# One attention kernel, one change: the output projection of an image spread one quarter at a time, and its group statistics by one selection product

## The chip, the cores and the metric

The kernel runs on one core of one Trainium2 chip. The metric is device time in microseconds (us) of one execution. The engines are TensorE (PE; its weight loads are PEld), VectorE (DVE), ScalarE (ACT), GpSimd (POOL) and SyncE (SP, which issues most DMAs). Each engine works through its own queue in order; they wait for one another by semaphores.

## The reference, cut to what matters

Eight images of 64 channels, 64 x 64. Four directional scans come first (not touched here). Then one attention layer:

```python
xn = group_norm(x, gn1_w, gn1_b)            # 32 groups of 2 channels
q, k, v = split(conv1x1(xn, w_qkv))         # 4 heads of 32
q, k = elu(q) + 1, elu(k) + 1
kv, k_sum = k^T v, sum of k                 # per head
out = (q kv) / (q . k_sum + 1e-6)
out = conv1x1(out, w_out)
out = group_norm(out, gn2_w, gn2_b)         # mean and variance over 2 channels x 64 x 64
return out + residual
```

The last group norm is what the change is about. A group is 2 channels; on the chip an image lies on 128 partitions (channel, and which half of the image), so the statistics of a group are spread over four partitions.

## The kernel before, in words

The scans end some 447 us into the program. Then comes a software pipeline of eight passes, one per image, by `iteration(b, par, cur, prev, pp)` on every engine (`batches` runs passes 0, 1, 2, a loop over 3 to 6, and 7), and a tail written out by hand. Pass b makes keys, queries and values of image b, denominators and outputs of image b-1 and, two behind, outputs and the last group norm of image b-2. The order on each queue is the order of the code; nothing else schedules it. Each pass has four quarters (i = 0 to 3), and a quarter is one chunk of 512 columns.

TensorE, per quarter: `token_major` (L595), `keys` (L603, L609), `queries` (L617, L621); one quarter later `gather` (L635) and `key_sums` (L641). In quarter 0 also `sums` (L650, L653) and `denominators` (L690). `output(c, cpar, i)` (L701) projects chunk i of image c; it needs the query units 2i and 2i+1 divided by their denominators (semaphore `normed`). Pass b runs outputs 2 and 3 of image b-2 in quarter 0, one on either side of `denominators`, and outputs 0 and 1 of image b-1 in quarter 3. `group_sums` (L666) adds the statistics over the four partitions of a group; it runs twice an image (mean, then variance), as `small(b, 3)` and `small(b, 4)`.

ScalarE: `tokens` (L1340), the exponentials of keys (L1374) and queries (L1380), `collect` (L1359), which copies a finished output chunk out of PSUM, `high_of` (L1335), and `affine` (L1394), the scale and shift of the last group norm over a whole image, in quarter 0 behind the collects.

VectorE: keys and queries finished (L1014, L1024), `small` (den_w and mix L1031/L1032, den L1036, reciprocal L1039), `normalise` (L1005), `low_half` (L287, two per pass, both at the end), `output_stats` (bn_stats L1063, two at a time) and the aggregate (L1057), and in `small(b, 3)` and `small(b, 4)` the deviations and the variance (L1044 to L1051).

SyncE: `broadcast(c, m)` writes the reciprocals of half m of image c to DRAM (`bounce`, L375) and reads them back over all partitions (four copies of 256 KB, L381). It issues the copies only when all units of image c-1 have been multiplied (`normed`).

GpSimd: `finish` (L479, residual added; waits for `affine`), `normalise_units` (L458, four units of 512 columns, first for half 0, then for half 1; each waits for its broadcast), `scale_and_shift` (L462, L466, L473: the inverse root, times weight, shift). "First units" below are those of half 0, "second units" those of half 1.

Of the kernel before, what the change touches and what calls it, by code (L numbers as in the profile page):

```python
# [53 lines left out]
SUBS = 4  # L54
SUB = CHUNK // SUBS
# [17 lines left out]
def constants():  # L73

    p = np.arange(P)
    head = p // DH
    group = (p % C) // 2
    row = np.arange(SUBS * DH)
    places = SUBS * head[:, None] + (row // DH)[None, :] == (row % DH)[None, :]

    sub, to = np.divmod(np.arange(SUBS * P), P)
    back = (p % DH)[:, None] == (SUBS * head[to] + sub)[None, :]
    return np.concatenate([np.eye(P), head[:, None] == head[None, :], (group[:, None] == group[None, :]) / 4.0,
                           places, back], axis=1).astype(np.float32)


def build(nc, x, k_td, k_dt, k_lr, k_rl, gn1_w, gn1_b, w_qkv, w_out, gn2_w, gn2_b, consts, out):
    with ExitStack() as ctx:
# [51 lines left out]
        back_to_heads = scan_rows[:, 0:SUBS * P].rearrange("p (s n) -> p s n", s=SUBS)  # L140
        back_ps = (key_ps[0], key_ps[1], query_ps[0], query_ps[1], acc_ps, out_ps, key_ps[0], tok_ps)
# [42 lines left out]
        dev2 = sb("dev2", [P, 4])  # L184
# [43 lines left out]
        normed_last, back_loaded, back_done = sem("normed_last"), sem("back_loaded"), sem("back_done")  # L228
        tail_done, tail_read = sem("tail_done"), sem("tail_read")
# [39 lines left out]
        def small_step(b, n):  # L269


            if isinstance(b, int):
                return n + 1 if b == 1 else 5 * b - 6 + n
            return b * 5 + (n - 6)
# [37 lines left out]
        def _(sp):  # L312
# [76 lines left out]

            for c in range(2):  # L390
                for m in range(2):
                    broadcast(c, m)
            sp.dma_start(back_to_heads, consts[:, 3 * P + SUBS * DH:].rearrange("p (s n) -> p s n", s=SUBS))\
# [25 lines left out]
        def _(pool):  # L419
# [41 lines left out]
            def scale_of_output(b, par):  # L461
                nc.gpsimd.tensor_tensor(scale2[:, par:par + 1], dev2[:, 1:2], half[:, 0:1], ALU.pow)\  # L462
# [6 lines left out]
            def scale_and_shift(b, par):  # L469
                scale_of_output(b, par)  # L470
                at_least(pool, scale_ready, 2 * b)
                settled(pool)
                nc.gpsimd.tensor_scalar(shift2[:, par:par + 1], dev2[:, 3:4], scale2[:, par:par + 1],  # L473
# [11 lines left out]
            def iteration(b, par, cur, prev, pp):  # L485
# [28 lines left out]
            pool.wait_ge(tail_read, 5)  # L514
# [6 lines left out]
            pool.wait_ge(tail_read, 7)  # L521
# [5 lines left out]
        def _(pe):  # L527
# [135 lines left out]
            def group_sums(v):  # L663
                for h in range(HEADS):
                    here = slice(h * DH, (h + 1) * DH)
                    last = nc.tensor.matmul(small_ps[here, 0:1], group_mean[:, here], v, start=True, stop=True)  # L666
                return last

            def small(b, n):
# [9 lines left out]
                if n >= 3:  # L679

                    at_least(pe, stat_ready, 2 * (b - 2) + n)
                    last = group_sums(agg2[:, 0:1] if n == 3 else dev2[:, 2:3])
# [22 lines left out]
            def iteration(b, par, cur, prev, pp):  # L705
                for i in range(4):
# [5 lines left out]
                    if i == 0 and prev:  # L712
                        small(b, 0)
                        if pp:
                            output(b - 2, par, 2)
                        else:
                            image_mean(0, REST, out_ps, rest_stat_ready, rest_stat_done)
                        denominators(b, par, 0)
                        if pp:
                            output(b - 2, par, 3)  # L720
                    if i > 0:
                        gather(b, i - 1)
                        if i == 3 and prev and has_next(b, cur):

                            at_least(pe, small_read, small_step(b, 0))
                            if not pp:
                                pe.wait_ge(rest_shift_ready, 1)
                            output(b - 1, 1 - par, 0)
# [5 lines left out]
                    if i == 3:  # L734
                        if pp:
# [726 lines left out]
```

## Time and profile before

| what | us |
|---|---|
| median of 3 runs | 667.25 (667.12 to 667.75) |
| the profiled execution | 667.11 |
| its span in the trace | 665.0 |
| the scans, up to pass 0 | about 447 |
| passes 1 to 7 | 466.3 to 635.0 |
| the tail | 635.0 to 665.0 |

Passes are told by ScalarE's first copy of the pass (acc_g, tok, L1345/L1340). The view by stretches gives, for each pass, its length, the busy time of each engine in it and TensorE's granted clock; the timeline gives single instructions with the idle time ahead of them and what ended it.

### The profile page before, as it was taken

The numbers are of one execution on the slowest core, as the hardware profiler recorded it, in microseconds if no ns is written. First come the engines' busy times: TensorE is split into PE (matmuls) and PEld (weight loads), VectorE is DVE, ScalarE is ACT, GpSimd is POOL, SyncE is SP. The second block draws the span as 40 slices with busy tenths as digits, with TensorE's granted clock in tenths as the row PEclk, the third lists the DMA queues.
The fourth block names the chain that finished last, engine by engine and source line by source line (L and its number), as shares of the span: only waits on it lengthen the run. The fifth ranks groups of instructions, "written<-read, shape, count | busy, mean of one in ns | idle before, by whom it ended". The sixth has DMA issues, their size and how long they took to land.

```text
span 665.0 us, 28191 instructions
## 1 busy us (share of the span) xinstructions
PE 624.7 (94%) x10787; PEld 535.6 (81%) x10787; DVE 568.4 (85%) x1945; ACT 430.2 (65%) x1062; POOL 135.2 (20%) x116
## 2 busy tenths in 40 slices
PE   8799999999999999999999999998989899899991
PEld 5799999999999899999999999965646555555550
DVE  5689989999989888989999999989878768778785
ACT  3456666677777766666665666657767767768744
POOL 0022200000000000000000000010164767767655
PEclk9999999999999999999999999999999999999996
DMA  9999990233333100000000000000326368368556
GB/s 173 206 203 189 166 178 1 51 82 80 80 79 83 41 1 0 0 0 0 0 2 0 0 0 0 0 1 2 73 69 148 78 134 177 90 132 178 111 91 130
DMA packets 79315, 50.40 MB, mean 76 GB/s; under 512 B 44256, under 2 KB 72352, under 8 KB 79264
## 3 DMA queue, kind: packets, MB, share of 16 engines
q1 hardware_dynamic: 75936, 48.91, 36.4%
q10 hardware_dynamic: 3328, 0.82, 0.6%
q8 instruction: 31, 0.51, 0.3%
q14 instruction: 20, 0.16, 0.1%
HBM read 32.34 MB, written 9.24 MB: 63 GB/s over the span
## 4 chain that ended last, share of the span: by engine, by line
PE 51%; DVE 19%; issue 10%; DMA 7%; POOL 6%; ACT 2%; SPq 1%; DVEq 1%; ACTq 0%; POOLq 0%
PE bank L554 44%; POOL rows_h L458 6%; DMA rows_h<-bounce 5%; DVE scan_rows L860 5%; DVE parts L860 3%; DVE parts L833 3%; DVE fin L947 3%; DMA bounce<-recip 1%; PE bank L635 1%; PE bank L701 1%; SPq L381 1%; DVE kp L1014 1%; DVE rows_h L1024 1%; DMA yn<-L_conv_k_td 1%; DVE recip L1039 1%
## 5 line engine op out<-in xcount | busy, mean ns | idle before, releaser
L554 PE MATMUL bank<-parts 128*128 128x124 f16 (+2 forms) x7560 | 421.3, 219 | 6.9 <-issue 3.7
L554 PEld LDWEIGHTS bank<-parts 128*128 128x128 f16 x7560 | 415.6, 98 | 13.0 <-issue 4.8
L1235 ACT ACTIVATE parts<-parts 128x128 f16<-128x128 f16 x506 | 156.6, 309 | 150.1 <-DVE parts L860 125.5
L833 DVE TENSOR_TENSOR parts<-scan_rows,parts 128x128 f16<-128x128 f32 x506 | 149.3, 295 | 14.2
L860 DVE SCALAR_TENSOR_TENSOR parts<-bank,cols_w 128x128 f16<-128x128 f32 x378 | 109.6, 290 | 21.7 <-PE bank L554 6.2
L860 DVE SCALAR_TENSOR_TENSOR scan_rows<-bank,cols_w 128x128 f32<-128x128 f32 x378 | 106.1, 281 | 0.0
L443 POOL TENSOR_TENSOR scale<-dev,half 128x2 f32<-128x2 f32 (+1 forms) x2 | 2.1, 1037 | 398.9 <-DVE dev L972 398.9
L458 POOL TENSOR_TENSOR rows_h<-rows_h 128x512 f32<-128x512 f32 x52 | 69.6, 1370 | 43.2 <-DMA rows_h<-bounce 43.2
L1014 DVE SCALAR_TENSOR_TENSOR kp<-ex,bank 128x512 f32<-128x512 f32 x64 | 41.0, 681 | 28.0 <-ACT ex L1374 27.5
L1246 ACT ACTIVATE cols_w<-scan_rows 128x256 f32 x126 | 52.5, 417 | 5.7 <-issue 0.2
L1374 ACT ACTIVATE ex<-bank,minus_one 128x512 f32<-128x512 f32 x64 | 40.5, 687 | 7.5 <-PE bank L609 7.1
L1380 ACT ACTIVATE ex<-bank,minus_one 128x512 f32<-128x512 f32 x64 | 40.7, 695 | 1.1 <-PE bank L621 1.1
L1024 DVE SCALAR_TENSOR_TENSOR rows_h<-ex,bank 128x512 f32<-128x512 f32 x64 | 40.9, 681 | 0.0
L860 DVE SCALAR_TENSOR_TENSOR parts<-bank,rows_h 128x128 f16<-128x128 f32 x124 | 36.0, 290 | 5.4 <-PE bank L554 0.4
L635 PEld LDWEIGHTS bank<-kp,tok 128*64 128x64 f32 x512 | 27.3, 136 | 11.3 <-issue 10.6
L1359 ACT ACTIVATE rows_h<-bank 128x512 f32<-128x512 f32 x26 | 15.6, 600 | 31.4 <-PE bank L701 29.2
L635 PE MATMUL bank<-kp,tok 128*64 128x128 f32 x512 | 35.0, 279 | 0.1
L860 DVE SCALAR_TENSOR_TENSOR scan_rows<-bank,rows_h 128x128 f32<-128x128 f32 x124 | 34.8, 281 | 0.0
L1262 ACT ACTIVATE cols_w<-ex 128x128 f32 (+1 forms) x84 | 34.0, 414 | 0.6 <-DMA ex<-scan_rows 0.5
L701 PE MATMUL bank<-rows_h,mix 128*64 128x512 f32 x96 | 25.4, 605 | 5.7 <-POOL rows_h L458 5.7
L947 DVE BATCH_NORM_STATS2 fin<-cols_w x96 | 28.8, 300 | 0.0
L1246 ACT ACTIVATE rows_h<-scan_rows 128x256 f32 (+1 forms) x64 | 26.7, 416 | 2.2
(143 smaller groups left out, 575.7 us busy)
## 6 DMA issues: line engine op xcount, KB each, us to landing
rows_h<-bounce SPq DMA_DIRECT2D x52, 256.0 KB, 4.9
cols_w<-x SPq DMA_DIRECT2D x6, 896.0 KB, 12.5
ex<-scan_rows SPq DMA_DIRECT2D x84, 64.0 KB, 2.0
out<-fin SPq DMA_DIRECT2D x10, 512.0 KB, 7.8
cols_w<-x SPq DMA_DIRECT2D x12, 384.0 KB, 9.2
cols_w<-x SPq DMA_DIRECT2D x12, 256.0 KB, 7.0
cols_w<-x SPq DMA_DIRECT2D x6, 512.0 KB, 10.7
kp<-scan_rows SPq DMA_DIRECT2D x40, 64.0 KB, 2.0
```

What stands on the lines that cost most here:

```text
L458: nc.gpsimd.tensor_tensor(qp[:, 1 - par, u, :], qp[:, 1 - par, u, :], recip_b[:, u, :], ALU.mult).then_inc(normed, 1)
L554: last = nc.tensor.matmul(conv_rows[g][u % SLOTS][:, :, to], w[:, k, d, :], rows_16[:, u % SLOTS, g * GB:(g + 1) * GB, of], start=part_n = ...
L635: nc.tensor.matmul(acc_ps[d * C:(d + 1) * C, 0:P], tok[:, i % 2, n * P + d * C:n * P + (d + 1) * C], kp[:, (2 * i + d) % 4, n * P:(n + 1) ...
L833: nc.vector.tensor_tensor(low[:, slot, gb, :], state[:, slot, gb, :] if row is None else row[:, gb, :], high[:, slot, gb, :], ALU.subtract ...
L860: nc.vector.scalar_tensor_tensor(out=to, in0=conv[g][u % SLOTS][:, 0:GB * J].rearrange("p (b j) -> p b j", b=GB), scalar=0.0, in1=add, op0 ...
L947: nc.vector.bn_stats(stats[:, b, bass.ds(n * 2 + (g - 2), 1), :].rearrange("p o s -> p (o s)"), cols[:, bass.ds(n * -BODY + (W + first), c ...
L1014: nc.vector.scalar_tensor_tensor(out=kp[:, m % 4, :], in0=ex[:, m % 2, :], scalar=1.0, in1=key_ps[m % 2][:, :], op0=ALU.min, op1=ALU.max)\
L1024: nc.vector.scalar_tensor_tensor(out=qp[:, par, u, :], in0=ex[:, 2 + u % 2, :], scalar=1.0, in1=query_ps[u % 2][:, :], op0=ALU.min, op1=AL ...
L1235: act.activation(high_down[:, slot, gb, :], high[:, slot, gb, :], ACT.Copy, scale=1.0 / LOW_SCALE).then_inc(down_ready[g], 1)
L1246: act.activation(to, state[:, slot, :, :], ACT.Copy).then_inc(saved, 1)
L1374: act.activation(ex[:, m % 2, :], key_ps[m % 2][:, :], ACT.Exp, bias=minus_one[:, :])\
L1380: act.activation(ex[:, 2 + u % 2, :], query_ps[u % 2][:, :], ACT.Exp, bias=minus_one[:, :])\
```

## The change

Six things change, all in the attention passes and the tail.

1. Outputs: pass b now runs output 0 of image b-1 in quarter 3, and outputs 1, 2 and 3 of image b-2 in quarters 0, 1 and 2 (before: 2 and 3 in quarter 0, 0 and 1 in quarter 3). The collects move with them. In quarter 3 both gathers stand ahead of both key sums.
2. Statistics: instead of two `group_sums` with VectorE work between them, `members()` multiplies the 24 columns of `stats2` (four bn_stats of six numbers) by four 0/1 matrices (`pick`), 16 matmuls of 24 columns, so that each partition gets all four members' bn_stats side by side in PSUM (96 numbers). One bn_aggr over the 96 (`joined`) gives mean and variance of the group; two one-column instructions make variance + eps and -mean.
3. GpSimd: `scale_and_shift` stands ahead of the second units. Its wait is for VectorE's two one-column results (`stat_ready`), which come at the end of the pass.
4. ScalarE: `affine` stands behind the exponentials of quarter 1 (before: of quarter 0).
5. VectorE: one `low_half` at the end of quarter 2, one at the end of quarter 3; bn_stats of chunks 0 and 1 in quarter 1 ahead of the second denominators, chunk 2 in quarter 2, chunk 3 in quarter 3 ahead of the queries.
6. One more DMA (`pick`, 256 KB) is issued by SyncE after the first image's broadcasts, and the tail uses `members` and `joined` in the place of the two sums.

```diff
+    member, to = np.divmod(np.arange(MEMBERS * P), P)
+    pick = p[:, None] == ((to % C) // 2 * 2 + member % 2 + member // 2 * C)[None, :]
...
             def scale_of_output(b, par):
-                nc.gpsimd.tensor_tensor(scale2[:, par:par + 1], dev2[:, 1:2], half[:, 0:1], ALU.pow)\
+                at_least(pool, stat_ready, 2 * b - 1)
+                nc.gpsimd.tensor_tensor(scale2[:, par:par + 1], dev2[:, 0:1], half[:, 0:1], ALU.pow)\
...
                 if prev:
                     normalise_units(b, par, 0)
+                if pp:
+                    scale_and_shift(b, par)
                 if prev and has_next(b, cur):
                     normalise_units(b, par, 1)
-                if pp:
-                    at_least(pool, small_read, small_step(b, 4))
-                    scale_and_shift(b, par)
...
-            def group_sums(v):
-                for h in range(HEADS):
-                    here = slice(h * DH, (h + 1) * DH)
-                    last = nc.tensor.matmul(small_ps[here, 0:1], group_mean[:, here], v, start=True, stop=True)
+            def members():
+                for j in range(MEMBERS):
+                    for h in range(HEADS):
+                        here = slice(h * DH, (h + 1) * DH)
+                        last = nc.tensor.matmul(small_ps[here, j * NCHUNK * 6:(j + 1) * NCHUNK * 6], pick[:, j, here],
+                                                stats2[:, :, :].rearrange("p n s -> p (n s)"), start=True, stop=True)
                 return last
...
+            def joined(b, read, n):
+                settled(dve)
+                nc.vector.bn_aggr(agg2[:, :], small_ps[:, 0:MEMBERS * NCHUNK * 6]).then_inc(read, 1)
+                at_least(dve, read, n)
+                at_least(dve, affine_ready, b - 1)
+                nc.vector.tensor_scalar(dev2[:, 0:1], agg2[:, 1:2], EPS_GN, None, ALU.add).then_inc(stat_ready, 1)
+                nc.vector.tensor_scalar(dev2[:, 1:2], agg2[:, 0:1], -1.0, None, ALU.mult).then_inc(stat_ready, 1)
...
+                    if i >= 2 and prev and has_next(b, cur):
+                        low_half(dve, b + 1, 1 - par, i - 2)
+                    if i == 3 and pp:
+                        small(b, par, 3)
...
                     if i == 0 and pp:
-                        collect(b - 2, par, (2, 3))
-                    if i == 0 and has_finished(b):
+                        collect(b - 2, par, (1,))
+                    if i == 1 and has_finished(b):
                         affine(b - 1, 1 - par, slice(0, J))
...
+                    if i in (1, 2) and pp:
+                        collect(b - 2, par, (i + 1,))
                 if prev and has_next(b, cur):
-                    collect(b - 1, 1 - par, (0, 1))
+                    collect(b - 1, 1 - par, (0,))
```

Where it moves instructions, at the three places that matter below. Line numbers are each kernel's own; ISA and REGISTER_ALU rows are semaphore and counter work.

GpSimd in the loop, one pass, before (fin: the residual; rows_h: units; scale, shift: the group norm's):

```order
L479 TENSOR_TENSOR fin<-rows_h,cols_w 128x64x32
L243 ISA
L458 TENSOR_TENSOR rows_h<-rows_h 128x512 x8
L243 ISA
L462 TENSOR_TENSOR scale<-dev,half 128x1
L243 ISA
L466 TENSOR_SCALAR scale<-scale,norm 128x1
L473 TENSOR_SCALAR shift<-dev,scale,norm 128x1
```

The same place now:

```order
L491 TENSOR_TENSOR fin<-rows_h,cols_w 128x64x32
L249 ISA
L468 TENSOR_TENSOR rows_h<-rows_h 128x512 x4
L249 ISA
L473 TENSOR_TENSOR scale<-dev,half 128x1
L477 TENSOR_SCALAR scale<-scale,norm 128x1
L485 TENSOR_SCALAR shift<-dev,scale,norm 128x1
L468 TENSOR_TENSOR rows_h<-rows_h 128x512 x4
```

The eight units are parted: the scale and shift stand between the first four and the second four.

ScalarE in the loop, from the first collect of a pass on, before (rows_h<-bank: a collect; 128x2048: the affine; tok and ex: tokens and exponentials):

```order
L1359 ACTIVATE rows_h<-bank 128x512
L243 REGISTER_ALU
L1359 ACTIVATE rows_h<-bank 128x512
L1394 ACTIVATE rows_h<-rows_h,shift,scale 128x2048
L243 REGISTER_ALU
L1340 ACTIVATE tok<-bank 128x512
L243 REGISTER_ALU
L1374 ACTIVATE ex<-bank,minus_one 128x512
L243 REGISTER_ALU
L1374 ACTIVATE ex<-bank,minus_one 128x512
L1380 ACTIVATE ex<-bank,minus_one 128x512 x2
```

The same place now:

```order
L1334 ACTIVATE rows_h<-bank 128x512
L249 REGISTER_ALU
L1315 ACTIVATE tok<-bank 128x512
L249 REGISTER_ALU
L1349 ACTIVATE ex<-bank,minus_one 128x512
L249 REGISTER_ALU
L1349 ACTIVATE ex<-bank,minus_one 128x512
L1355 ACTIVATE ex<-bank,minus_one 128x512 x2
L1371 ACTIVATE rows_h<-rows_h,shift,scale 128x2048
L249 REGISTER_ALU
L1334 ACTIVATE rows_h<-bank 128x512
```

Quarter 1's tokens and exponentials now follow one collect; the affine and the next collect follow them.

TensorE at the end of a pass in the loop, before (kp,tok: gather; rows_h,mix: output; kp,ones: key sums; agg/dev,cst: group sums):

```order
L701 MATMUL bank<-rows_h,mix 64x512 x2
L641 MATMUL bank<-kp,ones 32x256 x4
L243 REGISTER_ALU
L243 ISA
L666 MATMUL bank<-agg,cst 32x1 x4
L243 REGISTER_ALU x2
L635 MATMUL bank<-kp,tok 64x128 x8
L243 REGISTER_ALU
L701 MATMUL bank<-rows_h,mix 64x512 x2
L641 MATMUL bank<-kp,ones 32x256 x4
L243 REGISTER_ALU x2
L666 MATMUL bank<-dev,cst 32x1 x4
```

The same place now:

```order
L712 MATMUL bank<-rows_h,mix 64x512 x2
L249 REGISTER_ALU x2
L643 MATMUL bank<-kp,tok 64x128 x8
L649 MATMUL bank<-kp,ones 32x256 x8
L249 REGISTER_ALU
L675 MATMUL bank<-stats,scan_rows 32x24 x16
```

One output is left there, and the 16 matmuls with `pick` (L675) end the pass.

## Rows read from the trace of the kernel before

**Rows 1.** Stretches by pass (1, 2, 3, 6, 7): length, busy us, clock, DMA.

```profile
core 0: us, PE busy (x) PEld busy (x) DVE busy (x) ACT busy (x) POOL busy (x), PEclk, DMA share, GB/s
466.34:490.23 23.89, 21.64 (x366) 13.52 (x366) 19.43 (x35) 15.48 (x27) 8.51 (x7) 1.00 0.40 95
490.23:512.69 22.46, 22.46 (x386) 13.82 (x385) 18.49 (x34) 16.41 (x28) 9.05 (x8) 1.00 0.47 108
512.69:538.45 25.76, 23.00 (x386) 13.82 (x384) 19.13 (x35) 18.54 (x29) 17.05 (x13) 1.00 0.49 113
...
588.92:613.51 24.59, 22.92 (x386) 13.84 (x384) 19.45 (x35) 18.54 (x28) 17.65 (x13) 1.00 0.60 133
613.51:635.03 21.52, 20.50 (x361) 12.66 (x360) 16.65 (x31) 15.04 (x24) 15.59 (x12) 1.00 0.65 122
```

**Rows 2.** Timeline, GpSimd, pass 5 into 6: start, us, instruction, idle before.

```profile
568.95 0.57 POOL L462 TENSOR_TENSOR scale<-dev,half 128x1 f32<-128x1 f32 x1
...
570.25 1.38 POOL L473 TENSOR_SCALAR shift<-dev,scale,norm 128x1 f32<-128x1 f32 x1 [0.21 <-POOL scale L466]
574.04 4.58 POOL L479 TENSOR_TENSOR fin<-rows_h,cols_w 128x2048 f32<-128x2048 f32 x1 [2.42 <-ACT rows_h L1394]
579.52 4.99 POOL L458 TENSOR_TENSOR rows_h<-rows_h 128x512 f32<-128x512 f32 x4 [0.89 <-DMA rows_h<-bounce]
587.71 5.99 POOL L458 TENSOR_TENSOR rows_h<-rows_h 128x512 f32<-128x512 f32 x4 [3.20 <-DMA rows_h<-bounce]
```

**Rows 3.** Timeline, ScalarE, the same pass, quarters 0 to 1.

```profile
571.66 2.09 ACT L1394 ACTIVATE rows_h<-rows_h,shift,scale 128x2048 f32<-128x2048 f32 x1 [0.86 <-POOL shift L473]
573.66 0.58 ACT L1340 ACTIVATE tok<-bank 128x512 f32<-128x512 f32 x1
```

**Rows 4.** Timeline, VectorE, the same pass: quarter 1 and the end.

```profile
574.84 1.29 DVE L1014 SCALAR_TENSOR_TENSOR kp<-ex,bank 128x512 f32<-128x512 f32 x2 [3.43 <-ACT ex L1374]
...
577.71 0.95 DVE L1039 RECIPROCAL recip<-den 128x128 f32<-128x128 f32 x1
...
586.57 1.22 DVE L287 TENSOR_TENSOR parts<-yn,parts 128x1024 f16<-128x1024 f32 x1
...
588.45 1.61 DVE L287 TENSOR_TENSOR parts<-yn,parts 128x1024 f16<-128x1024 f32 x1
```

**Rows 5.** Timeline, SyncE's DMA issues, passes 2 and 5.

```profile
502.14 0.34 SPq L375 DMA_DIRECT2D bounce<-recip  x1
506.28 1.73 SPq L381 DMA_DIRECT2D rows_h<-bounce  x4
...
580.49 1.73 SPq L381 DMA_DIRECT2D rows_h<-bounce  x4
```

**Rows 6.** Timeline, TensorE: denominators of pass 6, and that pass's end.

```profile
592.39 1.08 PE L690 MATMUL bank<-rows_h,den_w 128*32 128x128 f32 x32
...
609.76 0.64 PE L641 MATMUL bank<-kp,ones 128*32 128x256 f32 x8
610.22 0.22 PE L666 MATMUL bank<-agg,cst 128*32 128x1 f32 x8
610.37 1.09 PE L635 MATMUL bank<-kp,tok 128*64 128x128 f32 x16
```

**Rows 7.** Groups by line and form: VectorE's aggregate of 78 and of 24 numbers.

```profile
L963 DVE BATCH_NORM_AGGREGATE agg<-fin 128x2 f32<-128x78 f32 x8 | 3.3, 469 | 0.0
...
L1057 DVE BATCH_NORM_AGGREGATE agg<-stats 128x2 f32<-128x24 f32 x8 | 2.1, 264 | 1.2 <-DVE stats L1063 0.2 <-DVE stats L1196 0.2
```

**Rows 8.** Timeline, GpSimd, the end of pass 7: scale and shift alone.

```profile
635.56 0.57 POOL L462 TENSOR_TENSOR scale<-dev,half 128x1 f32<-128x1 f32 x1 [1.08 <-DVE dev L1051]
...
636.84 0.33 POOL L473 TENSOR_SCALAR shift<-dev,scale,norm 128x1 f32<-128x1 f32 x1 [0.21 <-POOL scale L466]
```

**Rows 9.** Timeline, TensorE, the end of pass 1: its two outputs.

```profile
484.56 1.08 PE L701 MATMUL bank<-rows_h,mix 128*64 128x512 f32 x4 [0.93 <-POOL rows_h L458]
...
487.99 1.08 PE L701 MATMUL bank<-rows_h,mix 128*64 128x512 f32 x4 [0.76 <-POOL rows_h L458]
```

**Rows 10.** Timeline, VectorE, the tail: last aggregate and last variance.

```profile
652.11 0.26 DVE L1057 BATCH_NORM_AGGREGATE agg<-stats 128x2 f32<-128x24 f32 x1 [0.15 <-DVE stats L1196]
...
653.71 0.16 DVE L1147 TENSOR_SCALAR dev<-bank 128x1 f32<-128x1 f32 x1 [0.36 <-PE bank L666]
```

More of the change, by code:

```diff
@@ L54 @@
 SUBS = 4
+MEMBERS = 4
 SUB = CHUNK // SUBS
@@ L82, in constants @@
     back = (p % DH)[:, None] == (SUBS * head[to] + sub)[None, :]
+    member, to = np.divmod(np.arange(MEMBERS * P), P)
+    pick = p[:, None] == ((to % C) // 2 * 2 + member % 2 + member // 2 * C)[None, :]
     return np.concatenate([np.eye(P), head[:, None] == head[None, :], (group[:, None] == group[None, :]) / 4.0,
-                           places, back], axis=1).astype(np.float32)
+                           places, back, pick], axis=1).astype(np.float32)
 def build(nc, x, k_td, k_dt, k_lr, k_rl, gn1_w, gn1_b, w_qkv, w_out, gn2_w, gn2_b, consts, out):
@@ L678, in small @@
                     last = sums(small_ps)
-                if n >= 3:
-                    at_least(pe, stat_ready, 2 * (b - 2) + n)
-                    last = group_sums(agg2[:, 0:1] if n == 3 else dev2[:, 2:3])
+                if n == 3:
+                    if isinstance(b, int) and b == 2:
+                        pe.wait_ge(pick_loaded, 16)
+                    at_least(pe, norm2, b - 1)
+                    last = members()
                 last.then_inc(small_done, 1)
@@ L714, in iteration @@
                         if pp:
-                            output(b - 2, par, 2)
+                            output(b - 2, par, 1)
                         else:
@@ L718, in iteration @@
                         denominators(b, par, 0)
+                    if i in (1, 2):
+                        gather(b, i - 1)
                         if pp:
[L720 to L728, printed above, removed]
+                            output(b - 2, par, i + 1)
                         key_sums(i - 1)
@@ L734, in iteration @@
                     if i == 3:
+                        gather(b, 2)
+                        if prev and has_next(b, cur):
+                            at_least(pe, small_read, small_step(b, 0))
+                            if not pp:
+                                pe.wait_ge(rest_shift_ready, 1)
+                            output(b - 1, 1 - par, 0)
+                        gather(b, 3)
+                        key_sums(2)
+                        key_sums(3)
                         if pp:
                             small(b, 3)
-                        gather(b, 3)
-                        if prev and has_next(b, cur):
-                            output(b - 1, 1 - par, 1)
-                        key_sums(3)
-                        if pp and has_next(b, cur):
-                            small(b, 4)
             batches(pe, iteration)
```

105 lines of the change are left out of this document (35 added, 70 removed).

## The prediction, made before the changed kernel ran

> **What bounds the kernel now.** I read the stretches by pass first. Passes 3 to 6 last 25.76 us falling to 24.59 (they run from 512.69 to 613.51, 100.82 in all), while pass 2, whose TensorE work is the same, lasts 22.46 with TensorE busy in all of it [rows 1]. So TensorE's queue is worth about 22.5 us a pass, and passes 3 to 6 lose 2 to 3 us each to something that pass 2 lacks. VectorE, with 19.1 to 19.5 us of work, isn't it. The granted clock is 1.00 throughout, so the clock is out of it.
>
> What pass 2 lacks is ScalarE's affine. The timelines, read around it, give a ring. GpSimd ends the second units and starts the group norm's scale at 568.95; the shift ends at 571.63 [rows 2]; the affine runs from 571.66 to 573.75; only then come quarter 1's tokens [rows 3], and VectorE has stood 3.43 us for quarter 1's exponentials; its second reciprocal ends at 578.66 [rows 4]; the copies over the partitions are issued at 580.49 [rows 5]; GpSimd gets them at 587.71 and multiplies until 593.70 [rows 2], where the next scale starts. 593.70 - 568.95 = 24.75 us: scale and shift 2.7, affine 2.0, quarter 1 up to the reciprocal 5.0, the way through DRAM 9.0, units 6.0. That ring, not TensorE, is the pace.
>
> **What the change does to that ring.** It cuts it twice. The affine stands behind quarter 1's exponentials, so the shift no longer holds up that quarter; and the scale stands ahead of the second units. The affine's 2.09 us now lies ahead of quarter 2, where its cover is the 3.43 us that VectorE no longer loses a quarter earlier; with the collect behind it, it may make quarter 2 about a microsecond late, and VectorE has over 3 us a pass to spare against TensorE's 22.5.
>
> **What is late next.** Two candidates.
>
> TensorE: 22.46 us a pass, less two group sums, plus 16 matmuls. A group sum holds the queue from 610.22 to 610.37, 0.15 us, for 4 matmuls (8 records) [rows 6]; four times that is 0.6 us for 16. The other end is the denominators, also 16 matmuls of 32 output rows, but 128 columns wide: 1.08 us [rows 6]. 24 columns lie nearer to one column than to 128; I take 0.8 and keep 0.6 to 1.1. The queue is then 22.46 - 0.3 + 0.8 = 22.95 (22.75 to 23.25).
>
> A new ring through GpSimd. SyncE may issue the first copies of the next image only when all second units are multiplied, and these now stand behind the scale, which waits for VectorE's last instructions of the pass. From the end of the second units: copies until GpSimd starts, 587.71 - 580.49 = 7.2, and 0.2 for SyncE's wake; two first units, half of 4.99, 2.5 [rows 2, 5]; output 0, 1.0 [rows 9]; gather, 1.0, and two key sums, each 0.45 (609.76 to 610.22) [rows 6]; `members` 0.8; aggregate of 96 numbers, on the line through 264 ns for 24 and 469 for 78: 0.54 [rows 7]; variance 0.16 [rows 10]; four hand-overs at some 0.12, 0.5; scale to shift 1.6 (635.56 to 637.17) [rows 8]; second units 5.0. Sum 21.4. It turns in less than TensorE's queue, with 1.5 us to spare.
>
> That spare is what can be lost. VectorE's low part costs 1.22 us alone and 1.61 beside GpSimd's units [rows 4], and those four units take 5.99 there, 4.99 elsewhere; a shift beside VectorE takes 1.38 [rows 2], 0.33 alone [rows 8]. So each meeting of a unit with a low part (or with `normalise`) costs GpSimd 1.0 us. The change puts `normalise` in the second units' stretch and a low part in the first units' stretch. Neither need fall on the ring: a meeting with the last second unit or the third first unit delays nobody in it. The ring is 21.4 with none, 22.4 with one, 23.4 with two.
>
> On this meeting the Trainium skill ("SBUF — State Buffer", section "SBUF: two separate sides") says that VectorE's two-input or fast instructions and GpSimd share a port pair as an exclusive lock: who starts first keeps it, and the other stands fully. The 1.61 and 5.99 us agree (0.4 and 1.0 us of standing). By the page alone every overlap costs the rest of the other's instruction; by the rows, 1.0 us. Either way it speaks against this change, and leads to the second rival.
>
> I take a pass of 23.3 us: TensorE's 22.95 and 0.35 of waits. What in passes 3 to 6 is left of the ring's slack hides the rest: bn_stats moved by quarters, bn_stats ahead of the second denominators (two of them make the second reciprocal 1.2 us later, but the second units wait for the scale anyhow), and both gathers ahead of both key sums (same instructions).
>
> **The queues that are passed.** SyncE: the second half's bounce can now be issued while the first half's copies still fly. In pass 2 that happened: 502.14 to 506.28, 4.1 us until the copies could be issued, against 1.8 from the reciprocal's end (578.66) to 580.49 in pass 5 [rows 4, 5]. It makes a small ring of its own: 0.2 + 7.2 + 1.2 + 0.2 + 7.2 + 5.0 = 21.0 (1.2 being an estimate: bounce behind landed copies), also under TensorE. GpSimd: `finish` (4.58) stands behind the affine and ahead of the first units; it ends before the copies land, as in pass 5 (578.62 against 579.52) [rows 2]. The `pick` load is issued once, in passes where SyncE stands idle: nothing.
>
> **The sum**, against the profiled execution's 667.11 (2.11 us outside its span of 665.0; the median, 667.25, is 0.14 higher).
>
> - Passes 3 to 6: 100.82 becomes 4 x 23.3 = 93.2: -7.6 (91.2 to 97.6: -9.6 to -3.2).
> - Pass 1: the output at 487.99 leaves it, 1.0 us of work and 0.76 of wait: -1.8 [rows 9]. A low part, now at the end of quarter 2, may meet the first units and put the other output off by 1.0. I take -1.6 (-1.8 to -0.8).
> - Pass 2: it had no wait: 0.8 - 0.3 = +0.5 (+0.3 to +0.8).
> - Pass 7: gets a third output, 1.0, and `members` for a group sum, 0.65; its present 1.02 us without TensorE work (21.52 - 20.50) [rows 1] belongs to the old ring and goes: +0.6 (+0.4 to +0.9).
> - Tail: before, 652.11 to 653.87 from aggregate to variance, 1.76 us [rows 10]; now `members` 0.6 to 1.1, hand-overs 0.5, aggregate 0.54, variance 0.16: 1.8 to 2.3. The same step before it has cover in the last image's multiplications. +0.2 (0 to +0.5).
>
> -7.6 - 1.6 + 0.5 + 0.6 + 0.2 = -7.9: **659.2 us**. With the bounds of the forecast alone: 656.4 (all good ends) to 662.9 (23.8 a pass and all poor ends).
>
> **The rivals.**
>
> *TensorE isn't short at all.* The Trainium skill ("Perfetto Trace Analysis", section "Identifying the Most-Contended Engine") warns that TensorE's matmul busy share is no good measure of how near the limit it is, and wants the weight loads' share. That share is 13.82 of 22.46 us in pass 2 [rows 1]. If the 22.46 were a pace set by others, passes could come down to VectorE's 19.1 to 19.9. Against it: pass 2 shows TensorE without a single wait, which an engine that follows others doesn't show. It would give 4 x 20.5 = 82: 648. Chance 0.02.
>
> *The new ring sets the pace.* Two meetings and the 1.1 us `members`: 21.4 + 2.0 + 0.3 = 23.7, and a landing or hand-over later by 0.7: 24.4 a pass. 4 x 24.4 = 97.6, -3.2, and -0.3 for the rest: 663.6. For it: GpSimd is busy 17 to 18 us a pass and its queue order puts three waits in one line. Against: the meetings need exact places. Chance 0.20.
>
> *The gain is given back.* The ring at 25.2, as long as the pass now: 667. The scale's wait would have taken the affine's place. Chance 0.09.
>
> *Slower.* One mechanism: the second units, queued on GpSimd behind the wait for the pass's last VectorE instruction, hold back SyncE's first copies, and the first output of the next image holds TensorE. It decides from 25.3 us a pass on. Its price is 21.4 + three meetings, 3.0 (one in the second units, two in the first), + 1.05 for a shift beside VectorE (1.38 against 0.33) + 0.3: 25.8; 4 x 25.8 - 100.82 = +2.4, and -0.3 for the rest: 669.2. Against: the shift comes at the pass's start, some 4 us ahead of `normalise`. Chance 0.08.
>
> **How the numbers follow.** Forecast 0.61, at 659.2; rivals 0.02, 0.20, 0.09, 0.08. The likeliest case's own range is 656.4 to 662.9; to hold 8 in 10 the range takes in the ring at 24.4 with its poor ends: 656.4 to 664.8. About 0.2%, 1.3 us, is what a measurement can tell from no change: faster 0.82, same 0.10, slower 0.08.
>
> **What would show it.** In the changed trace: VectorE's wait of 3.4 us at quarter 1 gone; ScalarE's affine with no wait for the shift; passes 3 to 6 at 23 to 23.6 us with TensorE busy in nearly all; 32 records of the selection matmuls in 0.6 to 1.1 us; the aggregate near 0.54 us; GpSimd idle ahead of the scale (its wait for the pass's end) and the first units starting some 7.4 us after the second units end. I am wrong if TensorE waits over 1 us a pass for the first units at output 0 (the ring), or if VectorE waits for quarter 2's exponentials what it waited for quarter 1's.

## The result, and the profile after

The changed kernel takes 659.47 us (median of 4 runs, 659.12 to 660.12) where the kernel before takes 667.50 beside it: ratio 0.9871, interval 0.9841 to 0.9901. Measured a second time, beside other runs of before, it took 659.24 us, ratio 0.9882 (0.9854 to 0.9911). The forecast was 659.2, from 656.4 to 664.8. Two executions among the experiments below had a far lower mean granted clock (895.23 us at 0.655 in "before, affine in quarter 1", 788.47 us at 0.751 in "outputs and statistics"); the ratios leave them out, and they move those two medians by less than 0.1 us.

The first view is the changed kernel's stretches by pass (1 to 7, then the tail), columns as in [rows 1]:

```profile
core 0: us, PE busy (x) PEld busy (x) DVE busy (x) ACT busy (x) POOL busy (x), PEclk, DMA share, GB/s
468.53:491.40 22.87, 20.27 (x362) 13.54 (x362) 17.82 (x34) 14.87 (x25) 8.64 (x6) 1.00 0.47 110
491.40:514.03 22.63, 22.53 (x402) 14.07 (x402) 19.22 (x30) 16.48 (x28) 10.98 (x8) 1.00 0.47 109
514.03:537.20 23.17, 22.49 (x402) 14.00 (x400) 20.68 (x32) 18.25 (x29) 16.70 (x12) 1.00 0.52 120
537.20:561.08 23.88, 22.52 (x402) 14.07 (x400) 21.60 (x35) 18.24 (x29) 16.73 (x13) 1.00 0.66 141
561.08:584.07 22.99, 22.46 (x402) 13.98 (x400) 20.03 (x30) 18.24 (x29) 16.65 (x12) 1.00 0.66 144
584.07:607.12 23.05, 22.43 (x402) 14.09 (x400) 20.84 (x33) 18.24 (x29) 16.70 (x12) 1.00 0.68 142
607.12:628.03 20.91, 20.70 (x385) 13.01 (x384) 15.29 (x29) 15.62 (x24) 15.31 (x12) 1.00 0.62 121
628.03:657.40 29.37, 15.10 (x304) 7.89 (x290) 20.81 (x38) 13.39 (x20) 15.76 (x16) 0.84 0.65 120
```

Passes 3 to 6 came down from 100.82 us [rows 1] to 93.09, and TensorE is now busy in 22.4 to 22.5 us of each. Set against the forecast's terms, with both profiles of the changed kernel:

| stretch | before | forecast | first profile | second profile |
|---|---|---|---|---|
| up to pass 1 | 466.34 | 0 | +2.19 | +0.45 |
| pass 1 | 23.89 | -1.6 | -1.02 | -1.01 |
| pass 2 | 22.46 | +0.5 | +0.17 | +0.35 |
| passes 3 to 6 | 100.82 | -7.6 | -7.73 | -7.74 |
| pass 7 | 21.52 | +0.6 | -0.61 | -0.60 |
| tail | 29.97 | +0.2 | -0.60 | -0.65 |
| span | 665.0 | | 657.4 (-7.6) | 655.8 (-9.2) |

The profiled executions took 659.15 and 657.62 us, against 667.11 before. The second view is the timeline of pass 5 in the changed kernel (start, us, instruction, idle before it), which answers to [rows 2 to 6]:

```profile
561.05 0.56 POOL L473 TENSOR_TENSOR scale<-dev,half 128x1 f32<-128x1 f32 x1 [1.96 <-DVE dev L1052]
...
562.31 0.34 POOL L485 TENSOR_SCALAR shift<-dev,scale,norm 128x1 f32<-128x1 f32 x1 [0.20 <-issue]
562.60 4.97 POOL L468 TENSOR_TENSOR rows_h<-rows_h 128x512 f32<-128x512 f32 x4
571.99 4.59 POOL L491 TENSOR_TENSOR fin<-rows_h,cols_w 128x2048 f32<-128x2048 f32 x1 [4.41 <-ACT rows_h L1371]
576.60 5.97 POOL L468 TENSOR_TENSOR rows_h<-rows_h 128x512 f32<-128x512 f32 x4
...
569.59 2.11 ACT L1371 ACTIVATE rows_h<-rows_h,shift,scale 128x2048 f32<-128x2048 f32 x1
...
568.58 1.27 DVE L1016 SCALAR_TENSOR_TENSOR kp<-ex,bank 128x512 f32<-128x512 f32 x2
...
573.84 1.28 DVE L1016 SCALAR_TENSOR_TENSOR kp<-ex,bank 128x512 f32<-128x512 f32 x2 [0.32 <-ACT ex L1349]
...
567.53 0.34 SPq L381 DMA_DIRECT2D bounce<-recip  x1
569.34 1.74 SPq L387 DMA_DIRECT2D rows_h<-bounce  x4
573.70 0.34 SPq L381 DMA_DIRECT2D bounce<-recip  x1
576.78 1.73 SPq L387 DMA_DIRECT2D rows_h<-bounce  x4
...
580.14 1.08 PE L712 MATMUL bank<-rows_h,mix 128*64 128x512 f32 x4 [0.40 <-POOL rows_h L468]
...
582.91 0.47 PE L675 MATMUL bank<-stats,scan_rows 128*32 128x24 f32 x32
583.33 0.62 PE L603 MATMUL bank<-ident,parts 128*128 128x128 f16 x8
```

What to see: VectorE's `kp` of quarter 1 (568.58) carries no idle time, where it had 3.43 us [rows 4]; the affine (569.59) waits for nothing, and quarter 2's `kp` (573.84) waits only 0.32 us. (VectorE's longest wait for exponentials is now at quarter 0, 1.85 us at 562.88; TensorE has no marked wait there.) GpSimd waits 1.96 us for VectorE ahead of the scale and 4.41 us for the affine ahead of `finish`, which ends at 576.58, as the first units start. TensorE's only marked wait here is 0.40 us at output 0. The selection matmuls hold the queue from 582.91 to 583.33: 0.42 us.

### The profile page after: what moved, and what is told of

Read it like the earlier page. It is cut to its first block, busy times and chain, and to the rows that moved or that the text cites. A ratio compares the mean times of both kernels' runs of the same rounds, so it can differ in the third digit from the quotient of the medians.

```text
span 657.4 us, 28413 instructions
## 1 busy us (share of the span) xinstructions
PE 620.2 (94%) x10915; PEld 536.1 (82%) x10915; DVE 572.1 (87%) x1929; ACT 429.0 (65%) x1062; POOL 133.5 (20%) x116
## 4 chain that ended last, share of the span: by engine, by line
PE 63%; DVE 16%; issue 8%; POOL 5%; ACT 4%; DMA 2%; DVEq 1%; ACTq 0%; SPq 0%; POOLq 0%
PE bank L562 46%; DVE scan_rows L862 4%; DVE parts L862 3%; DVE fin L949 3%; PE bank L643 2%; PE bank L712 2%; POOL rows_h L468 2%; POOL fin L491 2%; DVE parts L835 2%; PE bank L617 2%; PE bank L649 2%; PE bank L603 2%; PE bank L629 1%; PE bank L701 1%; ACT ex L1349 1%
## 5 line engine op out<-in xcount | busy, mean ns | idle before, releaser
L862 DVE SCALAR_TENSOR_TENSOR parts<-bank,cols_w 128x128 f16<-128x128 f32 x378 | 109.7, 290 | 22.5 <-PE bank L562 7.0
L468 POOL TENSOR_TENSOR rows_h<-rows_h 128x512 f32<-128x512 f32 x52 | 71.7, 1410 | 19.4 <-DMA rows_h<-bounce 19.2
L643 PEld LDWEIGHTS bank<-kp,tok 128*64 128x64 f32 x512 | 28.8, 139 | 15.0 <-issue 13.5
L1315 ACT ACTIVATE tok<-bank 128x512 f32<-128x512 f32 x32 | 19.4, 605 | 15.4 <-PE bank L603 15.4
```

The costliest lines, as they stand in the source:

```text
L468: nc.gpsimd.tensor_tensor(qp[:, 1 - par, u, :], qp[:, 1 - par, u, :], recip_b[:, u, :], ALU.mult).then_inc(normed, 1)
L643: nc.tensor.matmul(acc_ps[d * C:(d + 1) * C, 0:P], tok[:, i % 2, n * P + d * C:n * P + (d + 1) * C], kp[:, (2 * i + d) % 4, n * P:(n + 1) ...
L862: nc.vector.scalar_tensor_tensor(out=to, in0=conv[g][u % SLOTS][:, 0:GB * J].rearrange("p (b j) -> p b j", b=GB), scalar=0.0, in1=add, op0 ...
```

## The experiments

Runs of one kernel scatter by one or two us, in one set by six. Pass 1 began between 465.4 and 468.5 us in the profiles: the first tokens of pass 0 came at 446.6 to 448.6, and pass 0 took 18.4 to 20.4. So beside each median I read two spans from the same trace: from the start of pass 1 to the end, and passes 4 to 6, which ran at full clock in all profiles but that of the outputs in pairs (last section).

| kernel | median us | pass 1 to end | passes 4 to 6 |
|---|---|---|---|
| before | 667.1 to 668.2 | 198.66 | 75.06 |
| changed, two profiles | 659.47, 659.24 | 188.87, 189.01 | 69.92, 69.89 |
| scale behind | 659.59 | 189.47 | 70.35 |
| affine in quarter 0 | 658.32 | 191.30 | 70.44 |
| leave early | 658.11 | 188.95 | 69.84 |
| before, affine in quarter 1 | 665.79 | 196.84 | 73.46 |
| outputs and statistics | 666.50 | 198.10 | 73.54 |
| outputs in pairs | 689.02 | 219.00 | 87.92 |
| output 0 later | 659.08 | 189.75 | 70.80 |
| low part later | 658.02 | 189.56 | 70.86 |
| low part behind statistics | 656.60 | 187.90 | 69.94 |
| low part and output 0 later | 659.02 | 189.33 | 70.86 |

### Which edit opened the ring

**Scale behind the second units again**, in the changed kernel:

```diff
-                if pp:
-                    scale_and_shift(b, par)
                 if prev and has_next(b, cur):
                     normalise_units(b, par, 1)
+                if pp:
+                    scale_and_shift(b, par)
```

> The changed kernel with one part undone: GpSimd's scale and shift stand behind the second units again. Theory G (the prediction's new ring: what TensorE waits for at output 0 runs through scale, second units and SyncE's leave to copy): the leave comes some 2 us earlier, the waits at output 0 (0.4 to 1.0 us in passes 3 to 6) go, passes 3 to 6 fall from 93.1 to about 91, time about 657.5. Theory R (the wait runs from the first reciprocal through DRAM to the first units, and the leave is there before the bounce has landed): nothing moves, since the affine, in quarter 1, needs the shift only some 6 us into the pass: passes 3 to 6 at 93 plus or minus 0.8, time 659 to 660.

659.59 us (658.49 to 660.13), ratio 0.9891 (0.9868 to 0.9914). Moving the scale is worth nothing that can be measured here: 0.1 us a pass.

**The copies leave without waiting for the second units**, in the changed kernel:

```diff
-                at_least(sp, normed, UNITS * c)
+                at_least(sp, normed, UNITS * c if m else UNITS * (c - 1) + 4)
```

> The changed kernel with one wait made weaker: SyncE issues the copies of the first reciprocals when the first units of the image before (not all units) have been multiplied. Theory G: as above, output 0 no longer waits, about 657.5. Theory R: no change, 659 to 660, and the waits at output 0 stay at 0.4 to 1.0 us.

658.11 us (656.82 to 659.44), 0.9872 (0.9848 to 0.9897). Passes 3 to 6 take 93.01 us, 0.08 less than in the changed kernel. SyncE's issues in pass 5 of this kernel show why:

```profile
565.21 0.35 SPq L381 DMA_DIRECT2D bounce<-recip  x1
567.05 1.74 SPq L387 DMA_DIRECT2D rows_h<-bounce  x4
```

The copies leave 1.84 us after the bounce, as in the changed kernel (567.53 to 569.34): they wait for the first reciprocal's way through DRAM, not for the second units. The new ring that I built on that leave isn't closed there; theory G falls, R stands.

**Affine at the end of quarter 0**, in the changed kernel:

```diff
-                    if i == 1 and has_finished(b):
+                    if i == 0 and has_finished(b):
                         affine(b - 1, 1 - par, slice(0, J))
```

> The changed kernel with one part undone: ScalarE's affine stands behind quarter 0's exponentials and collect again. If the affine's place by itself made the gain, quarter 1 comes 2 us late and passes 3 to 6 go back towards 25: 664 to 667. If the gain comes from the ring being open anywhere (the shift is there before the pass begins, so the affine waits for nothing), VectorE waits 1 to 2 us more at quarter 1, TensorE has that much to spare, and the passes stay at 23 to 23.5: 659 to 661.

658.32 us (657.02 to 659.62), 0.9868 (0.984 to 0.9896). With the scale early, the affine's place costs 0.2 us a pass. (Its longer sum, 191.3, is 1.6 us of slow clock in pass 1, where no affine is issued.) `finish` starts some 4 us earlier in the pass, and GpSimd then waits 2.8 to 3.9 us for the copies ahead of the first units, 13.7 us in passes 3 to 6: in the changed kernel `finish` and the copies end together, and freeing one alone does nothing.

**Only the affine's move**, put into the kernel before:

```diff
-                    if i == 0 and has_finished(b):
+                    if i == 1 and has_finished(b):
                         affine(b - 1, 1 - par, slice(0, J))
```

> The kernel before with one part of the change alone: the affine behind quarter 1's exponentials. If the old ring (second units, scale, affine, quarter 1, second reciprocal, DRAM, second units: 24.75 us) is what paced it, this cuts the affine and the scale out of it, some 4.7 us, TensorE becomes the pace, and passes 3 to 6 fall from 100.8 to 91 to 94: 658 to 661. If the spread outputs or the statistics are what gained, it stays at 665 to 667.

665.79 us, 0.9971 (0.9951 to 0.9991). The ring of the prediction is cut, and the 7.7 us of gain in passes 3 to 6 shrink to 1.4. Where it went is in TensorE's list of waits from 512 to 608 us, passes 3 to 6 but for the last microseconds (what it waited for: us in total, times, longest). The kernel before:

```profile
PE bank L603 <- DVE kp L1014: 4.0, 8, 0.6
PE bank L701 <- POOL rows_h L458: 3.6, 7, 1.0
```

With the affine moved:

```profile
PE bank L701 <- POOL rows_h L458: 7.2, 10, 1.7
```

The changed kernel:

```profile
PE bank L712 <- POOL rows_h L468: 2.4, 4, 1.0
```

The wait for quarter 1's keys is gone, and the outputs' wait for GpSimd's units has doubled (to the end of pass 6 it is 8.4 us, against 3.6). A second arm lay beside the affine: outputs 2 and 3 stand on TensorE behind the second units and ahead of quarter 1. Its timeline, pass 4 (GpSimd, TensorE, VectorE, SyncE):

```profile
538.99 5.96 POOL L458 TENSOR_TENSOR rows_h<-rows_h 128x512 f32<-128x512 f32 x4 [1.69 <-DMA rows_h<-bounce]
...
563.81 3.50 POOL L458 TENSOR_TENSOR rows_h<-rows_h 128x512 f32<-128x512 f32 x2 [1.87 <-DMA rows_h<-bounce]
...
545.10 1.08 PE L701 MATMUL bank<-rows_h,mix 128*64 128x512 f32 x4 [0.48 <-POOL rows_h L458]
...
551.63 0.95 DVE L1039 RECIPROCAL recip<-den 128x128 f32<-128x128 f32 x1
...
552.76 0.34 SPq L375 DMA_DIRECT2D bounce<-recip  x1
556.53 1.73 SPq L381 DMA_DIRECT2D rows_h<-bounce  x4
```

(The edge of the view cuts the second group of units to two.) From second units to second units 24.82 us, as in the old ring's 24.75: units 6.0, output 3 until 546.2, quarter 1 and the reciprocal until 552.58, the way through DRAM 11.2. That way took 9.0 before [rows 2, 4]: the second bounce now queues behind the first copies (552.76 to 556.53, 3.8 us), and part of what the affine gave back is lost there. GpSimd's first units end 1.87 us before those copies come, so without the queueing the turn could have been up to 1.9 us shorter, some 23 us (an estimate from these rows): the second arm is as long as the first only with the bounce behind the copies. The Trainium skill ("DMA: Bandwidth & Descriptors", section "Queues, rings and completion order") states that an engine's semaphore write lands only after every earlier write of that DMA engine; this row agrees, and so does 573.70 to 576.78, 3.1 us, in the changed kernel, against 1.8 for a bounce ahead of which no copies fly. Whether the bounce's data or only its semaphore write came late, the rows don't tell.

**Outputs and statistics alone**: the changed kernel with the scale behind the second units and the affine in quarter 0, both diffs from above together.

> The changed kernel with GpSimd's scale back behind the second units AND the affine back at the end of quarter 0; what stays of the change is one output per quarter and the statistics. Theory P (the prediction's ring, second units to scale to affine to quarter 1, was the pace): it is whole again, passes 3 to 6 back to 24 to 25 us each, 664 to 667 us. Theory O (the ring closed over outputs 2 and 3, which stood behind the second units and ahead of quarter 1 on TensorE; the affine lay beside it): 23.2 us a pass, 659 to 660 us. Theory T (both arms of the same length, either one closes the ring): 664 to 667 us, as P.

666.50 us, 0.9968 (0.9948 to 0.9988). The prediction's ring is back. Pass 5 to 6 of this kernel (GpSimd, ScalarE, VectorE):

```profile
564.43 4.98 POOL L468 TENSOR_TENSOR rows_h<-rows_h 128x512 f32<-128x512 f32 x4 [2.04 <-DMA rows_h<-bounce]
...
589.30 3.74 POOL L468 TENSOR_TENSOR rows_h<-rows_h 128x512 f32<-128x512 f32 x3 [3.45 <-DMA rows_h<-bounce]
...
572.00 2.10 ACT L1371 ACTIVATE rows_h<-rows_h,shift,scale 128x2048 f32<-128x2048 f32 x1 [3.54 <-POOL shift L485]
...
575.19 1.28 DVE L1016 SCALAR_TENSOR_TENSOR kp<-ex,bank 128x512 f32<-128x512 f32 x2 [3.43 <-ACT ex L1349]
```

(The edge of the view cuts the second group to three.) The turn is 24.87 us, with the affine's wait for the shift in it (3.54) and VectorE's 3.43 us at quarter 1 back, though the outputs no longer stand there. Theory T: either arm alone holds the pace at some 24.5 us.

**Outputs back in pairs**, in the changed kernel: TensorE issues 2 and 3 in quarter 0, 0 and 1 in quarter 3, with ScalarE's copies to match.

```diff
                         small(b, 0)
                         if pp:
-                            output(b - 2, par, 1)
+                            output(b - 2, par, 2)
...
                         denominators(b, par, 0)
+                        if pp:
+                            output(b - 2, par, 3)
                     if i in (1, 2):
                         gather(b, i - 1)
-                        if pp:
-                            output(b - 2, par, i + 1)
...
+                        key_sums(2)
                         gather(b, 3)
-                        key_sums(2)
+                        if prev and has_next(b, cur):
+                            output(b - 1, 1 - par, 1)
                         key_sums(3)
```

> The changed kernel with the outputs back in pairs: outputs 2 and 3 in quarter 0 and outputs 0 and 1 in quarter 3, their copies by ScalarE with them; scale, affine and statistics stay as changed. Theory P: the ring over scale and affine stays cut, 659 to 661 us. Theories O and T: quarter 1's keys stand behind output 3 and this behind the second units, passes 3 to 6 at 24 to 25 us, 664 to 667 us.

689.02 us (687.85 to 690.18), 1.0314 (1.0291 to 1.0337): far worse than either forecast. A longer ring closes; one turn in pass 5 (GpSimd, then TensorE):

```profile
576.60 4.97 POOL L468 TENSOR_TENSOR rows_h<-rows_h 128x512 f32<-128x512 f32 x4
588.98 4.59 POOL L491 TENSOR_TENSOR fin<-rows_h,cols_w 128x2048 f32<-128x2048 f32 x1 [7.40 <-ACT rows_h L1371]
593.51 6.93 POOL L468 TENSOR_TENSOR rows_h<-rows_h 128x512 f32<-128x512 f32 x4
603.57 0.57 POOL L473 TENSOR_TENSOR scale<-dev,half 128x1 f32<-128x1 f32 x1 [3.13 <-DVE dev L1054]
...
579.16 1.08 PE L712 MATMUL bank<-rows_h,mix 128*64 128x512 f32 x4 [1.67 <-POOL rows_h L468]
...
597.05 1.08 PE L712 MATMUL bank<-rows_h,mix 128*64 128x512 f32 x4 [2.04 <-POOL rows_h L468]
```

Second units (576.60), outputs 2 and 3, quarter 1, affine, `finish` (588.98), first units (593.51), outputs 0 and 1, `members`, scale (603.57), second units: the scale ahead of the second units puts a whole pass in one line once the outputs come in pairs. Pass 5, at full clock, takes 28.13 us.

Together: of the three cuts the spread outputs are needed, and of the other two either will do. "Needed" is in part read from a chain: no run has the outputs in pairs, the new statistics and the affine's move alone. "Before, affine in quarter 1" also has the old statistics and VectorE's old order; that it is the outputs that hold it is read from its turn above, in which output 3 lies and nothing of the statistics does. Passes 4 to 6, against 75.06 before: outputs spread with neither -1.5, affine late without the outputs -1.6, outputs with the affine late -4.7, outputs with the scale early -4.6, all three -5.1, scale early and affine late without the outputs +12.9 (three times pass 5, the one at full clock, would be +9.3).

### What is left in a pass

TensorE's queue is some 22.45 us and a pass 23.27 on average. TensorE's marked waits at output 0 come to 2.4 us in passes 3 to 6 (0.4 to 1.0 each) and to 2.0 us in pass 1.

**Output 0 later**, behind the fourth gather and the key sums:

```diff
                         gather(b, 2)
+                        gather(b, 3)
+                        key_sums(2)
+                        key_sums(3)
...
                             output(b - 1, 1 - par, 0)
-                        gather(b, 3)
-                        key_sums(2)
-                        key_sums(3)
```

> The changed kernel with output 0 moved behind the fourth gather and the key sums in quarter 3, some 2.3 us of TensorE's queue later. If the wait at output 0 (0.4 to 1.0 us a pass, 2.0 in pass 1) is all that lies between a pass and TensorE's queue of 22.45 us: passes 3 to 6 at 22.5 to 22.7 us, 655.5 to 657.5 us. If the queue is what the pass waits for at the end anyway (output 0's copy, the members and the next tokens come later by what is won): 659 to 661 us.

659.08 us (658.51 to 660.07), 0.9865 (0.9843 to 0.9887). Pass 1 takes 22.13 us, 0.74 less; passes 3 to 6 take 94.56, 1.5 more. The wait moves; this kernel's list of waits has, over passes 3 to 6:

```profile
PE bank L643 <- DVE kp L1016: 3.1, 4, 1.0
```

The fourth gather (not the third, as I wrote for a later run) now comes up on TensorE before VectorE has finished the keys of its own quarter, and what output 0 waited is waited there. The changed kernel's timeline has it ready to see: in passes 3 to 6 output 0 starts at 533.27, 556.76, 580.14 and 603.14, and the keys of quarter 3 end at 533.27, 556.68, 580.20 and 603.11.

**First low part behind the keys of quarter 3** instead of at the end of quarter 2:

```diff
+                    if i == 3 and prev and has_next(b, cur):
+                        low_half(dve, b + 1, 1 - par, 0)
                     if i == 3 and pp:
                         output_stats(b, par, (3,))
...
-                    if i >= 2 and prev and has_next(b, cur):
-                        low_half(dve, b + 1, 1 - par, i - 2)
+                    if i == 3 and prev and has_next(b, cur):
+                        low_half(dve, b + 1, 1 - par, 1)
```

> The changed kernel with VectorE's first low part moved from the end of quarter 2 to behind the keys of quarter 3, so that it no longer meets the first two of GpSimd's first units. Theory M (that meeting's 1 us is what TensorE waits for at output 0, 0.4 to 1.0 us a pass): passes 3 to 6 at 22.5 to 22.7 us, pass 1 shorter by 1, 655.5 to 657 us. Theory D (the low parts themselves are the next thing late, TensorE's tokens of the next pass wait for them): what is saved at output 0 is lost at the start of the pass, 659 to 661 us.

658.02 us (655.98 to 659.4), 0.984 (0.9809 to 0.987). Pass 1 takes 21.93 us, 0.94 less, where the first units take 6.0 us instead of 7.0; passes 3 to 6 gain nothing and take 1.3 us more (94.37).

**The same behind the last statistics**: as above, with `low_half(..., 0)` moved below `output_stats(b, par, (3,))`.

> The same without the move of output 0: the low part behind the last statistics, both right behind the keys of quarter 3. If only the members' wait for the statistics (0.8 us in one pass of four) is mended: 0.2 us a pass less than with the low part ahead of the statistics, 657 to 658.5 us.

656.60 us (656.25 to 657.28) beside the changed kernel's 659.24 (657.62 to 663.92) in the same comparison; 0.9829 (0.9808 to 0.985) of before. This is the lowest median of all versions. In the traces its gain over the change is 1.0 to 1.1 us from pass 1 to the end, in passes 1 (21.98) and 2 (22.36) and not in passes 3 to 6 (93.33); the rest of the 2.6 us between the two medians is not accounted for.

**Both moves**, the last one and output 0's:

> The changed kernel with three moves in quarter 3: VectorE takes the last statistics right behind the keys, then the first low part (from the end of quarter 2), then the queries; TensorE issues output 0 behind the fourth gather and the key sums. Each of the two single moves left what the other one takes away (with the low part moved, 0.8 us a time at output 0 and 0.8 us for the statistics; with output 0 moved, 0.6 to 1.0 us a pass at the third gather, for keys that stood behind the low part). If these waits are all: passes 3 to 6 at 22.5 to 22.8 us, pass 1 at 21.9, 654 to 656 us by the median. If the low parts become late for the next pass's tokens: 23.2 to 23.8 us a pass, 657 to 660 us.

659.02 us (657.96 to 659.72), 0.986 (0.9838 to 0.9882). The fourth gather still waits for `kp`, 0.6 to 1.0 us a pass, with the low part out of the way. Pass 4 of this kernel, quarter 3 (ScalarE, VectorE, TensorE):

```profile
550.72 1.92 ACT L1312 ACTIVATE parts<-yn 128x2048 f16<-128x2048 f32 x1
552.52 0.61 ACT L1336 ACTIVATE rows_h<-bank 128x512 f32<-128x512 f32 x1
552.99 0.62 ACT L1317 ACTIVATE tok<-bank 128x512 f32<-128x512 f32 x1
...
554.67 1.28 DVE L1016 SCALAR_TENSOR_TENSOR kp<-ex,bank 128x512 f32<-128x512 f32 x2 [2.36 <-ACT ex L1351]
...
556.09 1.09 PE L643 MATMUL bank<-kp,tok 128*64 128x128 f32 x16 [0.95 <-DVE kp L1016]
```

VectorE stands 2.36 us for the exponentials, and ScalarE comes to the tokens of quarter 3 only behind the high part and an output's copy, 1.4 us after TensorE has begun on them (551.63). So theory M holds for pass 1 alone. In passes 3 to 6 of the changed kernel the units for output 0 and the keys of quarter 3 are ready within 0.1 us of each other; here the units come first, and the keys, late with ScalarE's tokens, hold TensorE. That a pass of 22.5 us follows once both come earlier was not tried.

**The changed kernel again.**

> The changed kernel as it is, a second time. In its first profile TensorE's granted clock fell to 0.50 in pass 0 and pass 1 began at 468.5 us, while pass 1 of the seven other profiles read so far began at 465.4 to 467.0 at a clock of 1.00. If that fall was a matter of the one execution: pass 1 begins at 465.5 to 467, the span is 655 to 656.5 us, and the median 657.5 to 659.5 us. If the change itself brings it: the fall is there again, span 657 to 658 us.

659.24 us; in this profile pass 1 begins at 466.79, at full clock, and passes 1 to 7 and the tail agree with the first profile's within 0.2 us each.

## Why the prediction was right, and where it was not

The total held, in part by luck: an edit without a price did what the priced edits were credited with, and misses of size cancel. By its steps:

- **The pace.** The ring of 24.75 us was real: with the scale behind and the affine in quarter 0 it is there with the same 3.43 us at quarter 1. That it alone set the pace was wrong. "It cuts it twice" named two cuts of one arm, where one does (scale behind again, or affine in quarter 0 again: 0.1 to 0.2 us a pass). The step that failed is the edit I gave no price, one output per quarter: it takes outputs 2 and 3 from between the second units and quarter 1. The priced cut of the affine alone, without it, gains 1.4 us in passes 3 to 6, not 7.7. That the pass then falls to TensorE's queue was right.
- **Passes 3 to 6**: -7.6 forecast, -7.73 and -7.74 measured, from two sizes that were off. `members` hold TensorE 0.42 us, below my 0.6 to 1.1, so the queue is 22.45, not 22.95. The waits are 0.8 us a pass, not 0.35.
- **The new ring.** Rightly not the pace, but its first link was wrong: the copies wait for the reciprocal and the bounce. First units start 9.0 us after the second units end (567.57 to 576.60), not 7.4. The sign I gave against myself, over 1 us of wait a pass at output 0, didn't come in passes 3 to 6: 0.4 to 1.0 (2.0 in pass 1). The other, a long wait of VectorE at quarter 2, didn't either: 0.3.
- **`finish`** was said to end before the copies land. They end together, within some 0.5 us.
- **Meetings.** One a pass, in the first units (5.97 us, and 4.97 for the second), 1.0 us, as priced; two in pass 1 (7.0 us, and 6.5 in the second profile). That is why pass 1 gave 1.0 and not 1.6; it lies inside the bound.
- **Pass 2**: +0.5 forecast, +0.17 and +0.35 measured; the bound was +0.3 to +0.8.
- **Pass 7**: +0.6 forecast, -0.6 measured, outside the bound. With the same added work and the old ring whole (outputs and statistics alone) pass 7 takes 21.74, so the term that was mis-sized is the work: 0.2 more than before, not 1.65. Without the added work and with the affine late it takes 20.69, so the stalls that went were worth 0.8. TensorE's busy time rises from 20.50 to only 20.70 though it does an output more, which suggests that part of the old busy time was waiting too; subtracting the work from the idle 1.02 us missed that.
- **Tail**: +0.2 forecast, -0.6 measured. It is 29.27 to 29.38 in every kernel with the new statistics and 29.85 and 29.97 with the old, whatever the ring does, so the statistics gain it; 0.4 of it can be seen. From the last bn_stats to the scale's inputs it is 1.5 us (644.63 to 646.11) where the old way took 1.9; the aggregate of 96 numbers, which I put at 0.54, takes 0.59:

```profile
L1048 DVE BATCH_NORM_AGGREGATE agg<-bank 128x2 f32<-128x96 f32 x8 | 4.7, 592 | 1.6 <-PE bank L675 1.5
```

- **What cancelled.** From pass 1 on the change gave 9.8 us in the first profile, 1.9 more than forecast; 2.2 us were lost ahead of pass 1. Of these 1.6 are the clock in pass 0 (last section). Another 0.4 the change itself costs: pass 0, from its first tokens to those of pass 1, takes 18.39 us before and 18.82 in the second profile, where the fourth gather waits 0.56 us (464.11) for quarter 3's keys. "Both gathers ahead of both key sums (same instructions)" was put at nothing; with the old order, in outputs in pairs, it is 18.38. The second profile, without the clock's loss, took 657.62 us.
- **The range.** Its upper end, the ring at 24.4 with all poor ends, adds up to 665.3, not 664.8; nothing hangs on it.

## What to carry to other kernels

A ring read from one chain of waits may have a second arm of nearly the same length on another engine: before crediting an edit, list everything that stands between the same two events, and ask of each edit alone what the ring would be. When two versions differ by a microsecond, compare the stretches that the edit touches, not the medians; the rest of the program scatters by more. And once several engines arrive within half a microsecond of each other, moving one wait only shows the next.

## What the runs showed of the hardware

The granted clock fell after waits of TensorE of 1.3 to 2 us, in some executions and not in others. In pass 0 TensorE waits 1.32 us for VectorE in all thirteen profiles, the kernel before included; the clock fell there in two, the first profile of the changed kernel and that of the low part and output 0 later (pass 0 takes 20.39 us in both, against 18.82). The stretches of the changed kernel from 452 to 458 us, columns as in [rows 1], the clock third from the end. The first profile:

```profile
452.00:454.00 2.00, 0.86 (x6) 0.40 (x8) 2.00 (x3) 1.12 (x2) 0.00 (x0) 0.84 0.00 0
454.00:456.00 2.00, 2.00 (x16) 1.24 (x14) 1.95 (x4) 1.14 (x2) 0.00 (x0) 0.50 0.03 8
456.00:458.00 2.00, 2.00 (x26) 1.08 (x24) 2.00 (x5) 0.20 (x2) 0.00 (x0) 0.80 0.00 0
```

The second:

```profile
452.00:454.00 2.00, 1.04 (x10) 0.39 (x12) 2.00 (x3) 0.94 (x2) 0.00 (x0) 1.00 0.00 0
454.00:456.00 2.00, 2.00 (x32) 1.38 (x32) 2.00 (x5) 1.27 (x2) 0.00 (x0) 1.00 0.04 8
```

0.50 is 1.2 GHz, 1.00 is 2.4. Half as many matmuls start in the same two microseconds (16 against 32), and pass 1 begins 1.7 us later. Seven profiles have a 2.0 us wait at output 0 in pass 1, and in three of them the clock fell behind it: affine in quarter 0 and outputs and statistics (24.49 us each, against 22.87 with the clock at 1.00), and outputs in pairs. The same fall is in passes 3, 4 and 6 of the outputs in pairs, behind 2 us waits, and in pass 3 of outputs and statistics, behind a wait of 1.28. A wait on TensorE's queue can thus cost 1.6 us more than itself in one execution and not in the next; what decides it was not shown. Nor was it shown that the clock makes up the scatter of the runs without a trace: the mean granted clocks of the changed kernel's six, 0.988 to 0.992, don't follow their times.
